# Expert blocks that finish their own rows: the combination stage of a fused RWKV and mixture-of-experts layer moved into the loop over blocks

## The chip, the cores and the metric

One core of a Trainium2 chip runs the whole layer in one launch. The metric is the device time of that core in microseconds (us); lower is better. Engines: PE multiplies matrices, DVE (VectorE), ACT (ScalarE) and POOL (GpSimd) work on tiles of 128 partitions, SP only issues transfers.

## The reference, cut to what matters

`x` is 2 x 2048 x 256 in fp32, there are 8 experts with two matrices each (256x1024, 1024x256), and each token goes to its 2 best experts.

```python
x = _layernorm(x + attn(x))                      # WKV scan over time, projections
logits = einsum('bsd,de->bse', x, Wg) + bg
s, idx = top_k(logits, 2);  s = softmax(s)
h = einsum('td,edf->etf', tokens, W1) + b1       # even experts gelu, odd experts silu
y = einsum('etf,efd->etd', a, W2) + b2
out = einsum('te,etd->td', comb, y)              # comb: the two weights, 0 elsewhere
x = _layernorm(x + out)
```

## The kernel before, in words

**Stage A** walks over 8 chunks of 2 x 256 tokens. PE projects, DVE scans over time, ACT makes the exponents and gates, POOL writes the rows out. For every chunk DVE picks the two best experts of each token (`choose`), PE ranks the picks and DVE works out the slots (`place`); ACT normalises x1 into a record (`normalise_x1`), SP stores x1 (`x1_dram`) and POOL sends each token's record twice by indirect transfer, once into the region of each expert (`send_records`). A record is x1 (256 columns), a label that tells the row of the result, and the slot of the second pick.

**Block stage.** Regions are cut into blocks of 256 records. Two blocks of expert 0 run before the count is known (`early_products`); a small table on DVE (`row_t`, `ex_t`, `par_t`, `full_t`, after `cnt_done`) tells the others. Up to 41 blocks are possible, 35 are used with this input. For each block ACT loads the records, PE transposes them (`turn_records`), multiplies by W1 (`product1`, 48 matmuls), ACT applies gelu or silu, DVE makes the lower parts (`lower_parts`), PE multiplies by W2 (`product2`, two halves of 24 matmuls; the second is left out for a block with at most 128 records). Numbers are split in an upper and a lower part (fp32r), three matmuls for each product. At step t PE does `turn_records(t+2)`, `product1(t+1)`, `product2(t)`. DVE at step t: `outputs(t-1)` adds b2 and writes `y_sb`, then `halves(t+2)`, `lower_parts(t+1)`. POOL scatters the two halves of `y_sb` to `expert_out_dram` and, when an expert's last block is through, splits the weights of the expert after next (`split`, L576 and L580) into its slot of `wx`. ACT, DVE and POOL run this in a counted loop with a tail of branches, PE unrolled.

**Combination stage.** When all blocks are out, SP loads 16 pieces of 2 x 128 tokens, both expert outputs side by side; DVE and ACT weigh and add them to x1, DVE takes the statistics, POOL the inverse root, ACT normalises, SP stores.

All order is written by hand: each engine's queue is in order, and semaphores join them. The two places that matter most, DVE's step and the wait in PE's step:

```python
def block_step(t):        # DVE
    outputs(t - 1, expert); halves(t + 2, ...); lower_parts(t + 1)
...
pe.wait_ge(aTl_done, t.upto(FC // 2))            # PE, ahead of product2(t)
after(pe, y_done, (t - 1).upto(BH))
```

Of the kernel before, what the change touches and what calls it, by code (L numbers as in the profile page):

```python
# [23 lines left out]
ALU = mybir.AluOpType  # L24
# [8 lines left out]
P = 128  # L33
# [50 lines left out]
def build(nc, x, decay, first, mix_k, mix_v, mix_r, wkT, wvT, wrT, woT, w1, b1, w2, b2, wgT, bg, out):  # L84
# [18 lines left out]
    LOWER = 8  # L103
    REGION = TOKENS + BLK
    DUMMY = E * REGION
    REC = C + 2
# [3 lines left out]
    PIECES = T // P  # L110
# [8 lines left out]
    ys = nc.dram_tensor("expert_out_dram", (2 * TOKENS, C), F32, kind="Internal").ap()  # L119
    x1d = nc.dram_tensor("x1_dram", (B, T, C), F32, kind="Internal").ap()  # L120

    with ExitStack() as ctx:
# [31 lines left out]
        top2 = sb("top2", [P, NCH, J, 2])  # L154
        score = sb("score", [P, NCH * J, 2])
        score_t = sb("score_t", [P, NCH * J, 2])
# [47 lines left out]
        m8 = sb("m8", [P, J, 8], F32, phase_a)  # L204
        i8 = sb("i8", [P, J, 8], U32, phase_a)
# [44 lines left out]
        xx = sb("xx", [P, PIECES, B, C])  # L250
        phase_b = ExitStack()
        b2_b = sb("b2_b", [P, E * C], F32, phase_b)
        recs = [sb(f"recs{n}", [P, BH, REC], F32, phase_b) for n in range(RING)]
        dest = [sb(f"dest{n}", [P, BH], I32, phase_b) for n in range(RING)]
# [4 lines left out]
        y_sb = [sb(f"y_sb{n}", [P, BH, C], F32, phase_b) for n in range(RING)]  # L259
# [4 lines left out]
        yy = [sb(f"yy{n}", [P, B, 2 * C]) for n in range(RING)]  # L264
        zz = [sb(f"zz{n}", [P, B, C]) for n in range(RING)]
        res = [sb(f"res{n}", [P, B, C]) for n in range(RING)]
        y2 = [sb(f"y2_{n}", [P, B, C]) for n in range(RING)]
        stats_c = [sb(f"stats_c{n}", [P, B, 6]) for n in range(RING)]
        mv_c = [sb(f"mv_c{n}", [P, B, 2]) for n in range(RING)]
        rstd_c = [sb(f"rstd_c{n}", [P, B]) for n in range(RING)]  # L270
        shift_c = [sb(f"shift_c{n}", [P, B]) for n in range(RING)]

# [3 lines left out]
        bias1_done, top2_done = sem("bias1_done"), sem("top2_done")  # L276
# [27 lines left out]
        known, dest_done, rows_clear = sem("known"), sem("dest_done"), sem("rows_clear")  # L304
# [5 lines left out]
        y_out = [sem(f"y_out{n}") for n in range(RING)]  # L310
# [3 lines left out]
        mm2_done, y_done = [sem(f"mm2_done{n}") for n in range(BH)], sem("y_done")  # L314
        exp_done, score_done = sem("exp_done"), sem("score_done")
        yy_in = [sem(f"yy_in{n}") for n in range(RING)]
        res_out = [sem(f"res_out{n}") for n in range(RING)]
        xx_in, y2_done, c_sum2 = sem("xx_in"), sem("y2_done"), sem("c_sum2")
        c_sum, c_bn, c_mv, c_var, c_rstd, c_res = (sem(n) for n in ("c_sum", "c_bn", "c_mv", "c_var", "c_rstd", "c_res"))

        REC_DMAS = 2 * J * 16
        ROUTE1, ROUTE2 = 2 * J + 3, 7
# [6 lines left out]
        def blocks_in_line(body):  # L329

            for n in range(EARLY, BLOCKS + 1):
                body(Step(None, n, RING, BLOCKS))

        LAST = ALWAYS // RING * RING

        def blocks(eng, body):

            plain = lambda n: Step(None, n, RING, BLOCKS)
            for n in range(EARLY, RING):
                body(plain(n))  # L340
            with eng.Fori(1, LAST // RING) as m:
                for n in range(RING):
                    body(Step(m, n, RING, BLOCKS, LAST // RING))
            for n in range(LAST, BLOCKS + 1):
                body(plain(n))
# [7 lines left out]
        def if_used(eng, used, u):  # L353

            return eng.If(used > u.number) if u.largest >= ALWAYS else nullcontext()

        def pieces(eng, body):

            for n in range(RING):
                body(Step(None, n, RING, PIECES))  # L360
            with eng.Fori(1, PIECES // RING) as m:
                for n in range(RING):
                    body(Step(m, n, RING, PIECES))

# [1159 lines left out]
```

## Time and profile before

| | us |
|---|---|
| median of 3 runs (lowest, highest) | 746.29 (745.2, 747.39) |
| the profiled execution, its own time | 746.1 |
| its span, first to last instruction | 744.4 |
| busy in it: PE, DVE, ACT, POOL | 634.5, 458.6, 393.5, 304.6 |
| mean granted clock of PE | 0.926 |
| stage A until | about 265 |
| first block product starts | 265.0 |
| last matmul ends | 684.7 |

The busy share of an engine is a mean over stages with different limits, so it tells little alone. One reads which engine is never idle in a stage, and on which chain of waits the stage ends. A groups row gives busy time and mean length of one instruction; a timeline row gives start and length, and in brackets the idle time before and what ended it.

### The profile page before, as it was taken

Reading aid. Unit: us, or ns where it says so; the run is one execution under the profiler, and the core shown is the slowest. Engines: PE = TensorE matmul, PEld = TensorE weight load, DVE = VectorE, ACT = ScalarE, POOL = GpSimd, SP = SyncE. Lnnn points to the kernel's source line nnn. Section 1 sums busy time; section 2 is a strip of 40 time slices with the busy share of each in tenths; the row PEclk is TensorE's granted clock in tenths of the full one; section 3 lists DMA queues with packets and bytes.
Section 4 is the critical chain, followed back from the end, with each engine's and each line's share of the span. In section 5 each row is a group of like instructions: output and inputs, shape, how many; then the busy total and the mean of one; then the engine's idle time right before and its main releaser. Section 6 shows DMA issues by size and latency. Waiting matters only on the chain.

```text
span 744.4 us, 14706 instructions
## 1 busy us (share of the span) xinstructions
PE 634.5 (85%) x4472; PEld 592.7 (80%) x4472; DVE 458.6 (62%) x963; ACT 393.5 (53%) x715; POOL 304.6 (41%) x353
## 2 busy tenths in 40 slices
PE   5969799999974688999999999999999999997000
PEld 4858678788763588999999999999999999997000
DVE  4748879999999465564474654454544454432684
ACT  3545566676574151655454636646455463642474
POOL 5110115456446668255191461371821632122363
PEclk9998899999986789999999999999999999999555
DMA  8400212321224655934114151141151111100793
GB/s 253 131 29 1 85 39 98 106 100 58 82 91 130 200 180 134 350 98 158 44 44 165 35 164 38 48 142 60 36 171 45 38 44 52 37 28 31 260 307 119
DMA packets 57116, 78.75 MB, mean 106 GB/s; under 512 B 5190, under 2 KB 46611, under 8 KB 56884
## 3 DMA queue, kind: packets, MB, share of 16 engines
q1 hardware_dynamic: 41540, 51.59, 21.8%
q0 software_dynamic: 6496, 16.99, 6.4%
q10 hardware_dynamic: 8976, 8.72, 4.3%
q8 instruction: 73, 1.20, 0.7%
q14 instruction: 31, 0.25, 0.1%
HBM read 49.14 MB, written 28.92 MB: 105 GB/s over the span
## 4 chain that ended last, share of the span: by engine, by line
PE 72%; DVE 11%; issue 6%; ACT 5%; DMA 2%; POOL 2%; SPq 0%; ACTq 0%; DVEq 0%; POOLq 0%
PE hT_ps L869 27%; PE y_ps L878 26%; PE vr_ps L722 7%; PE k_ps L722 7%; PE xT_ps L887 2%; PE wo_ps L730 2%; DVE o_all L1214 2%; DMA yy<-expert_out_dram 1%; DVE xl L1292 1%; ACT L1017 1%; PE small_ps L744 1%; POOL rstd_c L689 1%; PE xT_ps L790 1%; DVE nd L1221 1%; ACT r L1017 1%
## 5 line engine op out<-in xcount | busy, mean ns | idle before, releaser
L869 PE MATMUL hT_ps<-xTh,wx 128*128 128x256 f32 x1120 | 211.3, 287 | 1.0 <-issue 1.0
L878 PE MATMUL y_ps<-wx,aTh 128*128 128x256 f32 x1088 | 198.7, 284 | 0.9 <-DVE y_sb L1200 0.9
L869 PEld LDWEIGHTS hT_ps<-xTh,wx 128*128 128x128 f32 x1120 | 178.2, 193 | 1.3 <-issue 1.2
L878 PEld LDWEIGHTS y_ps<-wx,aTh 128*128 128x128 f32 x1088 | 170.7, 193 | 1.1 <-issue 1.1
L1192 DVE TENSOR_TENSOR aTl<-hT_ps,aTh 128x512 fp32r<-128x512 f32 x140 | 93.1, 688 | 120.2 <-ACT aTh L1080 120.2
L670 POOL DMA_INDIRECT expert_out_dram<-y_sb,dest x70 | 68.3, 976 | 240.2 <-DVE y_sb L1200 224.5
L869 PE MATMUL hT_ps<-xTl,wx 128*128 128x256 f32 x560 | 159.1, 284 | 0.0
L878 PE MATMUL y_ps<-wx,aTl 128*128 128x256 f32 x544 | 154.5, 284 | 0.0
L1074 ACT ACT_TABLE_LOAD x33 | 42.3, 1283 | 170.8 <-PE hT_ps L869 159.9
L1074 ACT ACTIVATE hT_ps<-hT_ps,b_c 128x256 f32<-128x256 f32 x280 | 113.9, 469 | 19.7 <-DVE dest L1182 15.7
L869 PEld LDWEIGHTS hT_ps<-xTl,wx 128*128 128x128 f32 x560 | 108.3, 193 | 0.0
L878 PEld LDWEIGHTS y_ps<-wx,aTl 128*128 128x128 f32 x544 | 104.9, 193 | 0.0
L635 POOL DMA_INDIRECT records_dram<-rec,slot_i x64 | 74.9, 1170 | 62.3 <-DVE rec L1338 32.6
L722 PE MATMUL vr_ps<-xh,wq 128*128 128x512 f32 x256 | 85.6, 406 | 0.0
L1080 ACT ACTIVATE aTh<-hT_ps 128x512 fp32r<-128x512 f32 x140 | 84.2, 648 | 0.0
L1200 DVE TENSOR_TENSOR y_sb<-y_ps,b_b 128x256 f32<-128x256 f32 x70 | 29.3, 424 | 79.6 <-PE y_ps L878 77.7
L580 POOL TENSOR_TENSOR wx<-staging,wx 128x512 fp32r<-128x512 f32 x56 | 70.3, 1298 | 0.6
L722 PE MATMUL k_ps<-xh,wq 128*128 128x512 f32 x128 | 47.9, 448 | 16.0 <-DVE nd L1221 14.2
L722 PEld LDWEIGHTS vr_ps<-xh,wq 128*128 128x128 f32 x256 | 49.1, 192 | 11.3
L722 PE MATMUL vr_ps<-xl,wq 128*128 128x512 f32 x128 | 51.3, 401 | 0.0
L722 PEld LDWEIGHTS k_ps<-xh,wq 128*128 128x128 f32 x128 | 28.0, 219 | 24.1 <-issue 17.3
L730 PE MATMUL wo_ps<-wo,newton 128*128 128x256 f32 x128 | 34.1, 414 | 7.5 <-DVE newton L1242 5.0
(194 smaller groups left out, 850.0 us busy)
## 6 DMA issues: line engine op xcount, KB each, us to landing
staging<-in_L_ffn_W SPq DMA_DIRECT2D x16, 1024.0 KB
recs<-records_dram ACTq DMA_DIRECT2D x33, 258.0 KB, 2.8
yy<-expert_out_dram SPq DMA_DIRECT2D x16, 512.0 KB, 5.7
xin<-in_L_attn_x SPq DMA_DIRECT2D x16, 256.0 KB, 4.2
xres<-in_L_attn_x SPq DMA_DIRECT2D x16, 256.0 KB, 3.1
x_dram<-rec SPq DMA_DIRECT2D x16, 256.0 KB, 3.5
xx<-x_dram SPq DMA_DIRECT2D x2, 2048.0 KB, 22.1
out<-res SPq DMA_DIRECT2D x16, 256.0 KB, 4.0
```

The lines of the kernel that those rows point to most:

```text
L580: pool.tensor_tensor(wx[:, e % 2, 1, at], raw[:, at], wx[:, e % 2, 0, at].bitcast(F32), ALU.subtract).then_inc(weights_ready if n == LOWER ...
L635: pool.indirect_dma_start(xs, bass.IndirectOffsetOnAxis(ap=slot_i[at][:, n:n + 1], axis=0), rec[at][:, j, :], None, bounds_check=DUMMY - 1 ...
L670: pool.indirect_dma_start(ys, bass.IndirectOffsetOnAxis(ap=dest[t.slot][:, h:h + 1], axis=0), y_sb[t.slot][:, h, :], None, bounds_check=2 ...
L722: ins = pe.matmul(out_ps.rearrange("p (b t) -> p b t", b=B), wq[:, mat, now, part, cc, oc * P:(oc + 1) * P], xpart[c.slot][:, cc, :, now:n ...
L730: ins = pe.matmul(wo_ps[:, h, :], mixed[:, cc, b, h * P:(h + 1) * P], wo[:, cc, :], start=cc == 0, stop=cc == CC - 1)
L869: ins = pe.matmul(hT_ps[b][:, f, :], wx[:, s, part, off:off + P], xpart[t.slot % 2][:, cc, :], start=k == 0, stop=k == len(terms) - 1)
L878: ins = pe.matmul(y_ps[h], apart[t.slot % 2][:, fc, h * P:(h + 1) * P], wx[:, s, part, off:off + C], start=k == 0, stop=k == len(terms) - 1)
L887: ins = pe.transpose(xT2_ps[:, cc, h * P:(h + 1) * P], recs[u.slot][:, h, cc * P:(cc + 1) * P], ident[:])
L1074: act.activation(hT_ps[b][:, f, :], hT_ps[b][:, f, :], func, bias=b1_c[:, bass.ds(expert * FC + (2 * b + f), 1)]).then_inc(act_done, 1)
L1080: act.activation(aTh[u.slot % 2][:, 2 * b - 2:2 * b, :], hT_ps[b - 1][:], ACT.Copy).then_inc(aTh_done, 1)
L1192: dve.tensor_tensor(aTl[u.slot % 2][:, 2 * b:2 * b + 2, :], hT_ps[b][:], aTh[u.slot % 2][:, 2 * b:2 * b + 2, :].bitcast(F32), ALU.subtract ...
L1200: dve.tensor_tensor(y_sb[u.slot][:, h, :], y_ps[h], b2_b[:, bass.ds(expert * C, C)], ALU.add).then_inc(y_done, 1)
```

## The change

The combination goes away as a stage. A record now carries both slots' information and both weights (261 columns): label, first slot, the larger of the two slots, and two sigmoids of the score gap, made by ACT in stage A (`weigh`). A block's rows whose partner lies in a later block (`where_to[0]`) have their share, 2 x weight x (y + b2) + x1, stored to `x1_dram` by indirect transfer; rows whose partner was earlier (`where_to[1]`) gather the partner's share, add it, and are normalised with 4 x eps and scattered to `out`. The weight splits move from POOL to ACT (upper parts, 4 pieces) and DVE (lower parts, 4 pieces), behind the activations of an expert's first block. The counted loops are unrolled, and unused blocks lie in one nest of branches.

```diff
-    REC = C + 2
+    REC = C + 5
-    ys = nc.dram_tensor("expert_out_dram", (2 * TOKENS, C), F32, kind="Internal").ap()
...
+        def blocks_in_line(eng, used, lag, body):
+            with ExitStack() as needed:
+                for n in range(EARLY, BLOCKS + lag):
+                    if n - lag >= ALWAYS:
+                        needed.enter_context(eng.If(used > n - lag))
+                    body(Step(None, n, RING, BLOCKS))
...
@@ POOL
-            split(1)
+            for n in range(RING):
+                pool.memset(other[n][:], 0.0).then_inc(others_clear, 1)
...
+            def spread_z(t):
+                pool.wait_ge(mv_z_done, since_second(t) * BH)
...
+            def keep_shares(t):
+                pool.wait_ge(marks, t.upto(8))
+                pool.wait_ge(share_done, t.upto(BH))
...
+            def gather(t):
+                pool.wait_ge(marks, t.upto(8))
+                pool.wait_ge(share_out[(t - 1).slot], (t - 1).turn(16 * BH, 16 * BH))
...
+            def block_step(t):
+                for stage, u in ((keep_shares, t - 1), (send_rows, t - 2), (gather, t), (spread_z, t - 1)):
...
@@ PE
-                pe.wait_ge(y_done, early_block(0).upto(BH))
+                pe.wait_ge(share_done, early_block(0).upto(BH))
...
-                        after(pe, y_done, (t - 1).upto(BH))
+                pe.wait_ge(share_done, (t - 1).upto(BH, 1))
...
+                pe.wait_ge(share_done, (t - 1).upto(BH))
@@ ACT
+            def weigh(c):
+                at = c.number % RECS
+                act.wait_ge(gap_done, c.upto(1))
+                scattered(act, c)
+                act.activation(rec[at][:, :, C + 3], gap[:], ACT.Sigmoid, scale=-1.0).then_inc(weighed, 1)
+                act.activation(rec[at][:, :, C + 4], gap[:], ACT.Sigmoid).then_inc(weighed, 1)
...
+                if (i - 3).exists and i.number < NCH:
+                    weigh(i - 3)
                 if i.exists:
                     exponents(i)
...
+            def split_upper(t):
...
+                    act.wait_ge(raw_in, expert * 32 + 64)
+                    take_wait(act)
+                    for n in range(SPLITS):
...
+                        act.activation(wx[:, bass.ds(slot, 1), 0, at].rearrange("p a b -> p (a b)"), raw[:, at], ACT.Copy).then_inc(hi_done, 1)
...
@@ DVE
+            def mark(u, own):
...
+                dve.tensor_tensor(is_top[n][:], rows[:, :, C + 1], own, ALU.is_equal).then_inc(marks, 1)
...
+            def share_half(u, h, expert):
...
+                dve.tensor_tensor(y_ps[h], y_ps[h], b2_b[:, bass.ds(expert * C, C)], ALU.add).then_inc(y_done, 1)
+                dve.wait_ge(y_done, u.upto(BH, h + 1))
+                dve.scalar_tensor_tensor(out=share[u.slot][:, h, :], in0=y_ps[h], scalar=weight[u.slot][:, h:h + 1],
+                                         in1=recs[u.slot][:, h, 0:C], op0=ALU.mult, op1=ALU.add).then_inc(share_done, 1)
...
+            def add_other(u):
+                dve.wait_ge(other_in[u.slot], in_ring(u) * 16 * BH)
...
+                dve.tensor_tensor(row_out[u.slot][:], share[u.slot][:], other[u.slot][:], ALU.add).then_inc(sum_done, 1)
...
+            def normalise(u):
+                dve.wait_ge(rstd_z_done, since_second(u))
...
+                    dve.tensor_scalar(row_out[u.slot][:, h, :], row_out[u.slot][:, h, :], mv_z[u.slot][:, h, 0:1],
+                                      rstd_z[u.slot][:, h:h + 1], ALU.subtract, ALU.mult).then_inc(row_done, 1)
```

DVE's new step t is: second half of `share_of(t-1)`, `halves(t+2)` and `mark(t+2)`, `normalise(t-2)`, `lower_parts(t+1)`, `add_other(t-1)`, first half of `share_of(t)`, `split_lower(t)`. DVE in the block stage, one step of the kernel before:

```order
L1446 TENSOR_LOAD ex_t
L1446 ISA x2
L1199 REGISTER_ALU
L1200 ISA
L1200 TENSOR_TENSOR y_sb<-y_ps,b_b 128x256 x2
L1174 REGISTER_ALU
L1176 CAST xTh<-xT_ps 128x512
L1178 TENSOR_TENSOR xTl<-xT_ps,xTh 128x512
```

and the same place of the change, from the end of the marks to the start of the split (`TENSOR_LOAD` brings a number of a table into a register of the engine):

```order
L1181 SCALAR_TENSOR_TENSOR weight<-recs,twice 128x2
L1228 TENSOR_SCALAR row_out<-row_out,mv_z,rstd_z 128x256 x2
L1188 TENSOR_TENSOR aTl<-hT_ps,aTh 128x512 x4
L1216 TENSOR_TENSOR row_out<-share,other 128x512
L1219 BN_STATS stats_z<-row_out 128x6 x2
L1223 BN_AGGR mv_z<-stats_z 128x2 x2
L1209 TENSOR_LOAD ex_t
L1209 ISA x2
L1203 ISA
L1203 TENSOR_TENSOR y_ps<-y_ps,b_b 128x256
L1205 SCALAR_TENSOR_TENSOR share<-y_ps,weight,recs 128x256
L1494 TENSOR_LOAD split_t
```

Five kinds of work now stand in DVE's queue between two blocks where one stood, and there are three table loads in a step instead of one. ACT in stage A, chunks 3 to 7, the change:

```order
L940 ACTIVATE v<-vr_ps 128x512 x2
L969 ACT_TABLE_LOAD
L969 ACTIVATE rec<-gap 128x4
L970 ACTIVATE rec<-gap 128x4
L945 ACTIVATE B<-nd 128x4x256
L946 ACTIVATE A<-nd 128x4x256
L948 ACT_TABLE_LOAD
L948 ACTIVATE B<-B 128x4x256
```

Before, `B<-nd` followed `v<-vr_ps` directly and there was no table load ahead of `B<-B`: two table loads and two small activations are new, between the values and the exponents. DVE at the start of the block stage, the change, behind the lower parts of block 1 (12 more links of the table stand ahead of these, at L1461 to L1472, and 8 marks behind each `xTl`):

```order
L1203 TENSOR_TENSOR y_ps<-y_ps,b_b 128x256
L1205 SCALAR_TENSOR_TENSOR share<-y_ps,weight,recs 128x256
L1484 TENSOR_TENSOR wx<-staging,wx 128x1024 x4
L1188 TENSOR_TENSOR aTl<-hT_ps,aTh 128x512 x4
L356 TENSOR_LOAD ends
```

The lower weights of expert 1 were POOL's before; they now stand ahead of the lower parts of block 2.

## Rows read from the trace of the kernel before

**Rows 1.** Busy time by stretch: us, then each engine, clock, DMA share, GB/s.

```profile
300.00:685.00 385.00, 382.85 (x3200) 382.20 (x3198) 189.93 (x323) 204.12 (x422) 147.53 (x121) 1.00 0.27 86
684.80:744.40 59.60, 0.00 (x0) 0.00 (x0) 36.72 (x113) 30.55 (x64) 26.98 (x65) 0.54 0.66 218
```

**Rows 2.** The chain that ended last, in order of time: start, us, what.

```profile
300.86 5.76 PE hT_ps L869 x48
...
576.94 5.76 PE y_ps L878 x48
...
582.70 0.44 PE xT_ps L887 x4
...
686.07 2.29 DMA expert_out_dram<-y_sb,dest
```

**Rows 3.** Timeline of DVE, one block of the steady stage.

```profile
571.23 0.69 DVE L1176 CAST xTh<-xT_ps 128x512 fp32r<-128x512 f32 x1
...
572.56 0.34 DVE L1182 SCALAR_TENSOR_TENSOR dest<-recs,own_f 128x1 int32<-128x1 f32 x2
...
578.56 1.29 DVE L1192 TENSOR_TENSOR aTl<-hT_ps,aTh 128x512 fp32r<-128x512 f32 x2 [0.53 <-ACT aTh L1080]
580.03 0.42 DVE L1200 TENSOR_TENSOR y_sb<-y_ps,b_b 128x256 f32<-128x256 f32 x1 [0.18 <-PE y_ps L878]
```

**Rows 4.** Timeline of DVE in the combination stage.

```profile
696.41 0.74 DVE L1482 BATCH_NORM_STATS2 stats_c<-zz 128x6 f32<-128x256 f32 x2
697.08 0.67 DVE L1476 TENSOR_TENSOR zz<-zz,y 128x512 f32<-128x512 f32 x1
697.67 0.24 DVE L1490 BATCH_NORM_AGGREGATE mv_c<-stats_c 128x2 f32<-128x6 f32 x2
```

**Rows 5.** Timeline of DVE at the start of the block stage.

```profile
278.15 0.50 DVE L1417 TENSOR_TENSOR past_s<-past_s,rowbase 128x328 f32<-128x328 f32 x1
...
281.41 0.19 DVE L1429 TENSOR_SCALAR ex_t<-ex_f 128x41 int32<-128x41 f32 x1
...
281.93 2.48 DVE L1192 TENSOR_TENSOR aTl<-hT_ps,aTh 128x512 fp32r<-128x512 f32 x4
...
304.12 0.76 DVE L1200 TENSOR_TENSOR y_sb<-y_ps,b_b 128x256 f32<-128x256 f32 x2 [0.88 <-issue]
```

**Rows 6.** Timelines of ACT, then of DVE, in stage A.

```profile
164.43 0.60 ACT L973 ACTIVATE v<-vr_ps 128x512 f32<-128x512 f32 x1 [2.21 <-PE vr_ps L722]
...
189.35 0.60 ACT L973 ACTIVATE v<-vr_ps 128x512 f32<-128x512 f32 x1 [1.68 <-PE vr_ps L722]
190.87 1.07 ACT L978 ACTIVATE B<-nd 128x1024 f32<-128x1024 f32 x1 [0.92 <-DVE nd L1221]
...
169.44 1.22 DVE L1276 TENSOR_TENSOR b2v<-B,v 128x1024 f32<-128x1024 f32 x1
...
195.82 1.22 DVE L1276 TENSOR_TENSOR b2v<-B,v 128x1024 f32<-128x1024 f32 x1
```

**Rows 7.** Groups of POOL by line: count, busy us, mean ns, idle before.

```profile
L635 POOL DMA_INDIRECT records_dram<-rec,slot_i x64 | 74.9, 1170 | 62.3 <-DVE rec L1338 32.6 <-issue 25.0 <-DMA recs<-records_dram 3.8
...
L670 POOL DMA_INDIRECT expert_out_dram<-y_sb,dest x70 | 68.3, 976 | 240.2 <-DVE y_sb L1200 224.5 <-issue 15.3
...
L689 POOL TENSOR_TENSOR rstd_c<-var_e,half_neg 128x2 f32<-128x2 f32 x16 | 11.1, 696 | 1.3
```

**Rows 8.** Timeline of POOL: slow indirect issues of stage A, and two splits.

```profile
225.02 1.88 POOL L635 DMA_INDIRECT records_dram<-rec,slot_i  x1 [0.30 <-issue]
...
326.65 3.64 POOL L576 TENSOR_SCALAR wx<-staging 128x4096 fp32r<-128x4096 f32 x1
...
374.44 3.63 POOL L576 TENSOR_SCALAR wx<-staging 128x4096 fp32r<-128x4096 f32 x1
```

**Rows 9.** Timeline of ACT in the steady block stage.

```profile
572.74 1.28 ACT L1074 ACT_TABLE_LOAD   x1 [5.67 <-PE hT_ps L869]
...
577.86 1.16 ACT L1080 ACTIVATE aTh<-hT_ps 128x512 fp32r<-128x512 f32 x2
```

More of the change, by code:

```diff
@@ L351, in blocks_in_use, with if_used @@
             return eng.value_load(ends[0:1, E - 1:E], min_val=ALWAYS, max_val=BLOCKS)
[L353 to L363, printed above, removed]
-        def column(i, b, k):
-            at = (i.off // TH * J + b * TH + i.off % TH) * 2 + k
-            return at if i.fixed else i.m * (i.every // TH * J * 2) + at
+        def if_used(eng, used, u, known=0):
+            return eng.If(used > u.number) if u.number >= max(ALWAYS, known) else nullcontext()
         def after(eng, semaphore, value):
@@ new lines, in send_rows @@
+            def send_rows(t):
+                pool.wait_ge(row_done, since_second(t) * BH)
+                take_wait(pool)
+                for h in range(BH):
+                    pool.indirect_dma_start(
+                        rows_2, bass.IndirectOffsetOnAxis(ap=where_to[t.number % MARKS][:, 1, h:h + 1], axis=0),
+                        row_out[t.slot][:, h, :], None, bounds_check=TOKENS - 1, oob_is_err=False).then_inc(out_done[t.slot], 16)
+            keep_shares(early_block(0))
+            def block_step(t):
+                for stage, u in ((keep_shares, t - 1), (send_rows, t - 2), (gather, t), (spread_z, t - 1)):
+                    if u.exists and (with_second(u) or stage is keep_shares):
+                        with if_used(pool, used, u, t.number - 1):
+                            stage(u)
@@ L1452, in block_step @@
+                u = t - 2
+                if u.exists and with_second(u):
+                    with if_used(dve, used, u, known):
+                        normalise(u)
                 u = t + 1
                 if u.exists:
-                    with if_used(dve, used, u):
+                    with if_used(dve, used, u, known):
                         lower_parts(u)
-            blocks(dve, block_step)
-            dve.wait_ge(xx_in, 16 * B)
-            flat = score[:].rearrange("p n k -> p (n k)")
@@ L1492, in out_step @@
-            def out_step(i):
-                for stage, c in ((first_sum, i), (statistics, i - 1), (second_sum, i), (means, i - 1)):
-                    if c.exists:
-                        stage(c)
-            pieces(dve, out_step)
-            last = Step(None, PIECES - 1, RING, PIECES)
-            statistics(last)
-            means(last)
+                u = t - 1
+                if u.exists and with_second(u):
+                    with if_used(dve, used, u, known):
+                        add_other(u)
```

439 lines of the change are left out of this document (219 added, 220 removed).

## The prediction

> **What bounds the kernel now.** I read the busy times by stretch first, then the chain of waits, then the timelines of the engines that serve PE. Between 300 and 685 us PE works 382.85 of 385 us at full granted clock, while DVE has 189.93, ACT 204.12 and POOL 147.53 us of work [rows 1]: the block stage is PE's own time. The chain there runs through PE alone, and one block is 5.76 us of first product, 5.76 of second and 0.44 of transposes, 11.96 us (11.95 from block to block, as the starts in the chain say) [rows 2]. From the last matmul at 684.7 to the end at 744.4 PE has nothing to do: 59.6 us in which DVE, ACT, POOL and the transfers combine and normalise [rows 1]. That is what the change attacks. In stage A DVE is the engine that is hardly ever idle, so whatever is late there shows.
>
> **Part 1, the tail.** Removed: the 59.6 us. In its place stands what is still open when PE ends, with the last two blocks, 33 and 34. I count from the end of block 33's second product, at 677.9 in this trace (66.5 us before the end). In the kernel before, the last block then waited 0.9 us for `y_sb`; now only its second half waits for a share, so PE ends at about 5.9 instead of 6.8. POOL is the engine with the queue: an indirect issue is 0.98 us [rows 7] and 0.30 to the next ([rows 8] shows that gap), 1.28 each, two per stage. After block 33's share (1.3) it starts at about 2.2: keep_shares(33) to 4.8, send_rows(32) to 7.3, gather(34) behind the landing of the stores (about 2.3 us, [rows 2]) to 9.9, spread_z(33) (about 1.2, the power being 0.70, [rows 7]) to 11.2. The gather has landed by 12.2; DVE adds and takes statistics until 14.1. Then keep_shares(34) to 13.8, send_rows(33) to 16.3, spread_z(34) to 17.6, DVE normalises to 18.2, send_rows(34) issues to 21.3 and lands at 23.6. In the trace the last instruction ends some time after the last landing; I allow 1.7 us and get 25.3. 66.5 - 25.3 = **41.2 us saved**. Bounds: 30 us if each stage of POOL's queue takes 1.5 times as long, 46 if stages that I put in a row overlap.
>
> **Part 2, the steady block.** PE's matmuls are the same. The question is whether the engines that serve it keep within 11.95 us. DVE per block: two shares, each an addition of 0.42 [rows 3], 0.1 until its result is known, and a weighted addition of the same size, together 1.9; halves 1.33 (from the cast at 571.23 to the next operation at 572.56, [rows 3]); 8 marks on 2 columns at 0.12 each, as two small operations take 0.34 [rows 3], 1.0; normalisation, two of at most 0.42, say 0.6; four lower parts back to back 2.48 [rows 5]; adding the partner's share 0.67, statistics 0.74 and 0.24 with a wait, 1.8 [rows 4]. Sum **9.1 us**. Three loads of a register from a table are extra: mostly hidden, as 0.18 us of idle time before `y_sb` holds one [rows 3]; 0.88 us for two, where nothing hides them [rows 5]. So 9.1 to 10.4. ACT: a table load and activations from 572.74 to 579.0 [rows 9], 6.3 us, unchanged. POOL: six issues of 1.28 and 1.2 for the root, 8.9. All under 11.95: 0 us.
>
> An expert's split now costs ACT a table load of 1.28 and four copies of 128x1024 at about 1.07 [rows 6], 5.6 us, and DVE four subtractions of 1.22 [rows 6], 4.9, plus up to 1.3 for loads. There are six in the loop, 47.8 us or four blocks apart [rows 8]. In such a step DVE ends the split some 17 us after the step's start and the second share at 18.2; PE wants it at 21.0, and wants the lower parts of the block after next at 24.3 and has them by 23.7. Over four blocks DVE needs 4 x 9.1 + 4.9 = 41.3 us, at worst 4 x 10.4 + 6.2 = 47.8, of 47.8. So again **0 us**, and the cover is just used up at the worst end: if a DVE step takes 10.9, four blocks take 49.8, 2 us over, for six experts 12 us less what PE's slack hides.
>
> What goes away on POOL, the splits of 3.64 us and eight more pieces, held nothing on PE's chain: 0.
>
> **Part 3, stage A.** ACT's `weigh` stands between the copies of v and the exponents: 1.28 for the sigmoid's table [rows 9], about 0.3 for two tiny activations, and 1.28 more before the exponents. DVE's multiplication with the exponents starts at 195.82 and 169.44 [rows 6]. From 189.95 (v copied) the new order gives 191.5 for the start of `B<-nd`, two passes of 0.97, a table load and 1.05, so 195.8: just in time. In the other chunk v is copied at 165.03 and the exponents are there at 170.9, 1.5 us late. Of the five chunks two are like this one (1.5 and 0.8 by the same walk), three cost 0.1. With one more small operation on DVE per chunk (0.1): **+3.3 us**; bounds 0 (the copies of v slip ahead) and 8 x 1.6 = 13 (every chunk pays).
>
> **Part 4, the start of the block stage.** Marks of block 1 stand ahead of the last `choose`: 1.1 us, of which idle time covers half, +0.6. After the lower parts of block 1 (end 284.4, [rows 5]) DVE makes 12 more table steps: five of 246 elements at 0.44 (from 0.50 for 328, [rows 5]), seven small at 0.22 with their wait ([rows 5]: 0.19), 3.8 us; then two shares instead of two additions, to 290.1. Block 1's second product starts then, 2.8 us later than before. Behind it come the marks, the halves of block 3 (299.3), a share, the split of expert 1 (4.9 us, to 306.1) and only then the lower parts of block 2, the first at 306.8. PE's first product of block 3 started at 300.86 [rows 2] and needs that bank: 306.85. **+6.0 us**, and 0.5 for a lower clock after the idle time. ACT has by then made the upper parts (4.3 us in a gap that the pads' transfers leave open). Bounds 3 and 12.
>
> **The sum.** 744.4 - 41.2 + 3.3 + 0.6 + 6.5 = 713.6 us of span; the time is 1.7 over the span, **715 us**. The profiled execution (746.1) lies 0.2 under the median. Change: -31 us, -4.2%. A measurement of this kernel tells 0.3% (2.2 us) from no change.
>
> **The rivals.**
>
> *DVE becomes the bound, in part.* For: DVE's queue grows from about 6 to over 9 us a block, each step has three register loads and several waits on its own results, and a split comes on top. Against: its operations are timed above. At 10.9 us a step and 0 slack, 11 us are lost: 726. If every load cost 0.88 as in the idle row of [rows 5], 11.8 a step, four blocks with a split take 53.4, 5.6 over, six times, 34 us: 749, no gain.
>
> *POOL's queue becomes the bound: slower than before.* Six indirect issues a block instead of two, on an engine whose issues were 1.88 us while DVE worked on large operands in SBUF [rows 8], and 1.17 in the mean in stage A against 0.98 in the block stage, where DVE read PSUM [rows 7]. DVE now has additions, statistics and normalisations on SBUF in this stage. At 1.88 + 0.30 each and 1.2 for the root a block takes 14.3 us on POOL, 2.3 over PE's, for 32 blocks 75 us: 790. It decides from 11.95; it makes the kernel slower from 12.9 us a block. Against: DVE's SBUF operations are some 3 us of a block, not all of it, and gathers and scatters have 9 us of slack. The Trainium skill ("SBUF — State Buffer", section "Who interferes with whom") says that GpSimd and VectorE share one port pair as an exclusive lock, so that descriptors of transfers issued by GpSimd wait out a two-port VectorE operation. By that rule some issues lengthen by one such operation each, which speaks for this rival in kind; the rows of stage A agree in direction.
>
> *The weights come late.* The split moved from the end of an expert to ACT's and DVE's queues; if both fall behind, PE waits at each of six changes of expert, up to the 5 us of a split each: 745. Against: with four or five blocks per expert PE asks for them three steps later.
>
> The Trainium skill also has a price for a table switch ("ScalarE: Activation LUTs", section "What ACT_TABLE_LOAD costs"): 1283 ns and a drain of about 1380 ns, 2.66 us in all. The trace shows 1.28 and the next activation directly behind it [rows 9]. By the page's figure each of the two switches in stage A would cost 1.4 us more, some 14 us over five chunks, and the result would be 729.
>
> **How the numbers follow.** PE stays the bound, 705 to 722: 0.62. DVE partly the bound or the start dearer, 722 to 742: 0.22. Weights late, or DVE at its upper bound (745 to 749): 0.05. POOL the bound: 0.07. Something below 705: 0.04. The range, 706 to 738, leaves out half of that last one, the far end of the second case and the two dear rivals, about 0.19. Faster by over 0.3%: 0.87. Within 0.3%: 0.03. Slower: 0.10.
>
> **What would show it.** Right: PE busy without a gap between about 312 and 694 us, blocks 11.95 apart; under 20 us from the last matmul to the end; DVE at 75 to 90% in that stage; `weigh` costing at most 2 us in a chunk; first product of block 3 near 311. Wrong: PE waits for `share` or `aTl` in most blocks (DVE bound), `other` waited for by DVE and POOL never idle (POOL bound), waits at the first block of each expert (weights).

## The result, and the profile after

The changed kernel takes 774.43 us (median of 4 runs, 770.35 to 775.89) against 746.84 for the kernel before beside it (745.2 to 749.0): a ratio of **1.036, interval 1.031 to 1.041**. It is slower. The forecast was 715, range 706 to 738, with 0.87 on faster. The profiled execution took 775.44 us, its span 773.6, mean clock 0.906. In two of the five groups of runs below everything took longer, the kernel before included (753.0 and 755.5 us instead of 744 to 747); these runs are marked "disturbed", and every ratio is against the kernel before of the same group.

The busy time by stretch, columns as in [rows 1]:

```profile
300.00:685.00 385.00, 347.83 (x2774) 341.04 (x2774) 269.53 (x714) 209.58 (x398) 182.28 (x205) 0.94 0.25 78
685.00:749.00 64.00, 60.59 (x506) 59.19 (x504) 43.24 (x118) 28.79 (x61) 37.29 (x43) 1.00 0.19 54
749.00:773.60 24.60, 0.00 (x0) 0.00 (x0) 4.08 (x11) 0.00 (x0) 11.38 (x14) 0.60 0.12 40
```

The tail behaves: 24.6 us behind the last matmul where 59.6 stood. But PE, which never paused between 300 and 685 us before, now works 347.8 of 385 us, part of it at a lower clock. What PE waits for from 300 us on (us in total, times, longest), from the list of waits:

```profile
PE xT_ps L857 <- DMA recs<-records_dram: 32.7, 10, 6.0
PE hT_ps L839 <- issue: 3.8, 10, 0.7
PE hT_ps L839 <- DVE aTl L1188: 2.1, 1, 2.1
PE y_ps L848 <- DVE share L1205: 1.4, 1, 1.4
```

Neither DVE nor POOL is named much. Ten waits, eight of them of 1.4 to 6.0 us and two under 0.4, are for the **load of the records**, of which the prediction says nothing. ACT's timeline at the first of the six splits in the loop (start, us; in brackets the idle time before):

```profile
344.61 1.16 ACT L1058 ACTIVATE aTh<-hT_ps 128x512 fp32r<-128x512 f32 x2
345.47 0.39 ACTq L1044 DMA_DIRECT2D recs<-records_dram  x1
348.06 1.28 ACT L1083 ACT_TABLE_LOAD   x1 [2.29 <-issue]
349.35 3.90 ACT L1083 ACTIVATE wx<-staging 128x1024 f32 x4
353.27 1.28 ACT L1052 ACT_TABLE_LOAD   x1
...
358.40 1.16 ACT L1058 ACTIVATE aTh<-hT_ps 128x512 fp32r<-128x512 f32 x2
359.28 0.39 ACTq L1044 DMA_DIRECT2D recs<-records_dram  x1
```

and the chain of waits right behind it:

```profile
359.28 7.89 DMA recs<-records_dram
367.21 1.11 PE xT_ps L857 x4
```

The load is issued at 359.28, takes 7.89 us instead of about 3, and PE starts its transposes at 367.21. They take 1.11 us instead of 0.44 [rows 2], since the clock has fallen. The granted clock of the idle stretch, of the transposes and of the first 3 us of the product behind them (last column but two) is 0.78, then 0.50, the lower of its two levels, 1.2 GHz:

```profile
361.20:367.20 6.00, 0.01 (x1) 0.00 (x0) 3.80 (x10) 0.00 (x0) 1.76 (x3) 0.78 0.72 244
367.20:368.30 1.10, 1.08 (x4) 0.71 (x4) 0.92 (x2) 0.00 (x0) 1.02 (x1) 0.50 0.00 0
368.30:371.30 3.00, 2.99 (x15) 2.96 (x15) 2.77 (x12) 0.00 (x0) 2.47 (x4) 0.50 0.09 25
```

The eight first products behind the waits of 1.4 to 6.0 us, and one behind the wait of 2.1 us for lower parts, take 7.1 to 8.0 us instead of 5.9.

The change also moves the load within ACT's step, which the excerpt of the diff ahead of the prediction does not show:

```diff
 def block_step(t):          # ACT
-    u = t + 3
-    ...
-            after(act, dest_done, (u - RING).upto(BH))
-            load_records(u)
     u = t + 1
     ...
             activate_block(u)
+    u = t + 3
+    ...
+            after(act, share_done, (u - RING).upto(BH))
+            load_records(u)
+    split_upper(t)
```

In both traces a load follows directly on an activation, so ACT's timeline looks the same. The difference is which block it carries. Before, the load behind the activation of block k was for block k+3, which PE turns 15.5 us after the issue; now it is for k+2, turned one block of 11.95 us sooner, some 3.5 us after the issue. A landing takes 2.8 us in the median before, so there is next to nothing left for a late ACT or a busy transfer.

Of the feared costs, the groups show little (busy us, mean ns, idle before):

```profile
L631 POOL DMA_INDIRECT x_dram<-share,where_to x70 | 72.7, 1038 | 162.1 <-issue 147.2
L642 POOL DMA_INDIRECT other<-x_dram,where_to x64 | 67.7, 1057 | 39.0 <-issue 39.0
L651 POOL DMA_INDIRECT out<-row_out,where_to x64 | 62.8, 981 | 22.7 <-issue 16.8
L1203 DVE TENSOR_TENSOR y_ps<-y_ps,b_b 128x256 f32<-128x256 f32 x70 | 30.2, 431 | 56.6 <-issue 52.9
```

POOL's indirect issues are 0.98 to 1.06 us, where [rows 7] had 0.98. DVE stands 52.9 us ahead of 56 shares, 0.94 us each: loading the expert's number is not hidden, though I had taken it as mostly hidden.

### The profile page after: what moved, and what is told of

Same layout as the page of the kernel before. It is cut to its first block, busy times and chain, and to the rows that moved or that the text cites. A ratio compares the mean times of both kernels' runs of the same rounds, so it can differ in the third digit from the quotient of the medians.

```text
span 773.6 us, 14838 instructions
## 1 busy us (share of the span) xinstructions
PE 659.2 (85%) x4472; PEld 608.2 (79%) x4472; DVE 550.3 (71%) x1398; ACT 414.1 (54%) x709; POOL 352.8 (46%) x424
## 3 DMA queue, kind: packets, MB, share of 16 engines
q1 hardware_dynamic: 28708, 34.85, 13.8%
## 4 chain that ended last, share of the span: by engine, by line
PE 50%; ACT 14%; issue 13%; DVE 9%; DMA 7%; ACTq 3%; POOL 1%; SPq 0%; POOLq 0%; DVEq 0%
PE hT_ps L839 17%; PE y_ps L848 12%; PE vr_ps L692 8%; DMA recs<-records_dram 7%; PE k_ps L692 6%; ACT hT_ps L1052 5%; PE wo_ps L700 3%; PE xT_ps L857 2%; PE small_ps L714 2%; ACT aTh L1058 2%; ACT wx L1083 2%; DVE o_all L1242 1%; ACT L1052 1%; DVE xl L1320 1%; PE xT_ps L760 1%
## 5 line engine op out<-in xcount | busy, mean ns | idle before, releaser
L839 PE MATMUL hT_ps<-xTh,wx 128*128 128x256 f32 x1120 | 222.5, 297 | 6.3 <-issue 3.8
L848 PE MATMUL y_ps<-wx,aTh 128*128 128x256 f32 x1088 | 194.4, 281 | 4.4 <-DVE share L1205 4.4
L839 PEld LDWEIGHTS hT_ps<-xTh,wx 128*128 128x128 f32 x1120 | 187.1, 202 | 11.9 <-issue 9.3
L839 PE MATMUL hT_ps<-xTl,wx 128*128 128x256 f32 x560 | 164.6, 294 | 0.0
L631 POOL DMA_INDIRECT x_dram<-share,where_to x70 | 72.7, 1038 | 162.1 <-issue 147.2
L1052 ACT ACTIVATE hT_ps<-hT_ps,b_c 128x256 f32<-128x256 f32 x280 | 113.7, 465 | 20.4 <-PE hT_ps L839 18.7
L839 PEld LDWEIGHTS hT_ps<-xTl,wx 128*128 128x128 f32 x560 | 113.4, 202 | 0.0
L642 POOL DMA_INDIRECT other<-x_dram,where_to x64 | 67.7, 1057 | 39.0 <-issue 39.0
L651 POOL DMA_INDIRECT out<-row_out,where_to x64 | 62.8, 981 | 22.7 <-issue 16.8
L1203 DVE TENSOR_TENSOR y_ps<-y_ps,b_b 128x256 f32<-128x256 f32 x70 | 30.2, 431 | 56.6 <-issue 52.9
L857 PE MATMUL xT_ps<-ident,recs 128*128 128x128 f32 x132 | 22.7, 300 | 34.8 <-DMA recs<-records_dram 34.8
```

The costliest lines, as they stand in the source:

```text
L631: pool.indirect_dma_start(rows_1, bass.IndirectOffsetOnAxis(ap=where_to[t.number % MARKS][:, 0, h:h + 1], axis=0), share[t.slot][:, h, :], ...
L642: pool.indirect_dma_start(other[t.slot][:, h, :], None, rows_1, bass.IndirectOffsetOnAxis(ap=where_to[t.number % MARKS][:, 1, h:h + 1], ax ...
L651: pool.indirect_dma_start(rows_2, bass.IndirectOffsetOnAxis(ap=where_to[t.number % MARKS][:, 1, h:h + 1], axis=0), row_out[t.slot][:, h, : ...
L839: ins = pe.matmul(hT_ps[b][:, f, :], wx[:, s, part, off:off + P], xpart[t.slot % 2][:, cc, :], start=k == 0, stop=k == len(terms) - 1)
L848: ins = pe.matmul(y_ps[h], apart[t.slot % 2][:, fc, h * P:(h + 1) * P], wx[:, s, part, off:off + C], start=k == 0, stop=k == len(terms) - 1)
L857: ins = pe.transpose(xT2_ps[:, cc, h * P:(h + 1) * P], recs[u.slot][:, h, cc * P:(cc + 1) * P], ident[:])
```

## The experiments

There were eighteen runs. Labels in brackets are those of the disturbed ones. All edits of a disturbed run were run again undisturbed, but for f1 and f2.

| run | edit | ratio [interval] |
|---|---|---|
| c0 | the changed kernel again | 1.039 [1.035, 1.043] |
| c3 | kernel before, load behind the activation | 1.049 [1.046, 1.052]; disturbed (e3): 1.056 |
| e7 | kernel before, loops unrolled | 1.001 [0.998, 1.003] |
| e6 | changed, weights' transfer cut to 8 KB pieces | 1.003 [1.001, 1.005] |
| e5 | changed, split cut to 8 columns | 1.013 [1.010, 1.016] |
| c4 | changed, no sigmoid | 1.032 [1.029, 1.034]; disturbed (e4): 1.107 |
| d1 | changed, load first | 1.120 [1.115, 1.125]; disturbed (e1, c1): 1.124, 1.125 |
| f1 | changed, six buffers | disturbed: 1.123 |
| c2 | load first and six buffers | 0.980 [0.976, 0.984]; disturbed (e2): 1.036 |
| f2 | c2 and one register load a block | disturbed: 1.031 |
| b1 | f2, start mended, sigmoid moved | 0.977 [0.974, 0.979] |
| d2 | b1 without the moved sigmoid | **0.957 [0.954, 0.960]**; disturbed (b2): 1.025 |

**A control (c0).** The changed kernel, unaltered, since the first four runs (e1 to e4) had been disturbed.

> The changed kernel itself, unaltered, beside the three runs that follow. Reason: in the four runs before this one the kernel before took 753 us instead of 747, and ScalarE and VectorE stood idle for 1.5 to 3.8 us at places where nothing they need was missing, which the changed kernel's first trace does not show. If that is a matter of where the program's instructions lie (each edit moves them), this run looks like the first one: ratio 1.03 to 1.04, no such idle stretch. If it is a matter of the chip that ran them, the ratio is above 1.06 here too, and the runs before must be read against this one.

1.039, with 31.8 us of waits for records in ten places and no idle stretch without a cause: the first result repeats. That the disturbance does not come from where the instructions lie is shown by the programs that ran both ways (e3 and c3, e4 and c4, e2 and c2, b2 and d2).

**The move alone, in the kernel before (c3).** The three statements of the diff above change places, nothing else.

> The kernel before with the load of records behind the activation, again, for the same reason. In the first call it was 1.0555, with 18.8 us of PE waits for records in ten places. Theory: on an undisturbed chip the waits remain, since they come from the order alone: at the changes of expert, where the weights' transfer shares the way, and after blocks with at most 128 records; 1.01 to 1.04. If it is 1.00, the order costs nothing in the kernel before, and the loss of the changed kernel needs the split in front of the load as well.

Measured 781.67 us against 744.41, 37 us more. PE's waits from 300 us on:

```profile
PE xT_ps L887 <- DMA recs<-records_dram: 18.7, 9, 3.9
PE hT_ps L869 <- issue: 6.2, 12, 0.7
```

This is more than I expected (1.01 to 1.04), and more than the net loss of the changed kernel. By their places they come at the start (a landing of 6.7 us, issued at 305.47), at the changes of expert and behind half blocks. The waits are 25 us; most of the rest is five first products of 7.5 to 8.2 us and slow transposes behind them. So the split on ACT is not needed for a loss of this kind; the order does it.

**Unrolled code (e7).** A rival formed after the result: the loops of ACT and DVE are written out block by block, and instructions run once must be fetched.

```diff
-            with eng.Fori(1, LAST // RING) as m: ...
+            for n in range(EARLY, BLOCKS + 1):
+                body(Step(None, n, RING, BLOCKS))
```

> Another part of the change alone, in the kernel before: the counted loops of ScalarE and VectorE over the blocks are written out block by block (ScalarE's program grows from 1382 to 2786 instructions, VectorE's from 1076 to 1442). Theory A (the load of records one step late, and the loop of waits behind it, is the whole loss): no difference, within 0.5% of the kernel before, and no PE wait over 1 us. Rival theory B (instructions that are executed once must be fetched, and the engines stand while they are: the changed kernel's programs for ScalarE and VectorE are 3784 and 3463 instructions long): idle stretches of 1.5 to 3.8 us marked as issue or as an unknown releaser appear on ScalarE and VectorE inside a block, PE loses some of them where they come late in a block, and the kernel is 1 to 5% slower.

744.76 against 745.19: nothing, and no PE wait over 0.9 us from 300 us on. The fetches are there, as the page's queue rows show (packets, MB, share), of the kernel before, of this run, of the changed kernel:

```profile
q14 instruction: 31, 0.25, 0.1%
```

```profile
q14 instruction: 45, 0.37, 0.2%
```

```profile
q14 instruction: 63, 0.52, 0.2%
```

The fourteen more of the second row cost nothing, in straight code. The Trainium skill ("Runtime: NRT & Kernel Launch", section "Instruction fetch mechanics") says so too: fetching is sequential and mostly hidden, and a taken branch out of the window is what stalls. This trace agrees as to the first half.

**What lengthens the landing (e6).** The raw weights of experts 3 to 7 are loaded as two pieces of 8 KB instead of two of 1 MB, so this kernel leaves out most of them.

```diff
+                if e > 2:
+                    for n in range(2):
+                        sp.dma_start(raw[:, 16*n:16*n+16], w1[e][0:P, 0:16]).then_inc(raw_in, 16)
+                    return
```

> The changed kernel, with the two 1 MB loads of each expert's raw weights, from expert 3 on, cut to 8 KB each (so the weights that are split are not those experts'). Theory A: the weights' transfer is what makes the landing of the records take 7 to 8 us instead of 3.2 in the steps that follow a split; the six waits of about 6 us shrink to about 1.5, and with the clock that comes back the kernel gets 25 to 35 us faster than the run of the changed kernel beside it. If the landing stays at 7 us or the waits stay, the transfer is not what delays it, and ScalarE's late issue behind the split is the cause by itself: under 10 us.

746.08 us, 27 less than the changed kernel beside it (772.96). From issue to landing of the records, first the changed kernel, then this run:

```profile
DMA to landing us min/median/max: 2.7/3.4/7.7
```

```profile
DMA to landing us min/median/max: 2.7/2.9/3.8
```

and PE's waits fall from 31.8 us to

```profile
PE xT_ps L861 <- DMA recs<-records_dram: 12.1, 10, 2.5
```

The 2 MB of weights are asked for when DVE ends its split, three microseconds ahead of the late load (356.60 and 359.28 at the first split), and the two meet: in the changed kernel the five loads behind such a transfer land after 6.0 to 7.9 us. This is within the expectation.

**What the split itself costs (e5).** All pieces of the split, on ACT and DVE, cut from 1024 to 8 columns, so most of the weights are not split.

```diff
-                        at = bass.ds(n * WE // SPLITS, WE // SPLITS)
+                        at = bass.ds(n * WE // SPLITS, 8)
```

> The changed kernel, with every piece of the six splits in the block stage cut from 1024 to 8 columns on ScalarE and VectorE (the weights that are not split are left as they were before; the branches, loads of numbers and table loads of the split stay). Theory A: 3.9 us less in ScalarE's queue and 4.6 in VectorE's at each of six experts, so the load of the records after a split goes out 3.9 us earlier, but collides with the raw weights' transfer as before: the waits of 6 us fall to 2 to 3, 15 to 25 us faster than the changed kernel beside it. If the kernel gets less than 6 us faster, the splits on these two engines cost nothing, as part 2 of the prediction had it.

754.33 us, 18.6 less than the changed kernel: within the expectation. The waits for records are 17.0 us in 8 places. The cut works in two ways that this run does not separate. At the first split the load of the records goes out at 357.38 instead of 359.28, and it lands in 6.26 us instead of 7.89, the weights being asked for at 353.09 instead of 356.60.

**The load first (e1, c1, d1), buffers (f1), both (e2, c2).** The load's place is undone:

```diff
+                load_records(t + 3)          # with its wait
                 activate_block(t + 1)
-                load_records(t + 3)
                 split_upper(t)
```

> One part undone: in ACT's step the load of the records for three blocks ahead stands ahead of the activation of the next block again, as it does in the kernel before; everything else is the changed kernel. Theory (the load is issued too late: PE waits 32.7 us for records in the block stage and then pays again in clock): the load is issued about 6 us earlier in each step, so nearly all waits of xT_ps for records should go, 32.7 us down to under 10, and the time should fall from 774 to about 725 to 740; some is left because the load now waits on ACT for a share that DVE finishes late in a split step. Rival (DVE and ACT are the bound through splits and register loads): PE would wait for hT or share instead, and the time would stay above 765. Rival (the records wait for memory that other transfers hold): landings stay near 8 us in split steps, waits of 2 us at each of six experts, about 755.

This fell: 1.124 and 1.125 in the disturbed e1 and c1, far slower. The trace of e1 gave a ring of waits, which I then forecast for an undisturbed run:

> The load first with four buffers. If the ring of waits (activation, last lower part, partner's sum, two shares, load) holds, most blocks are 14.6 us apart whatever the time of day: ratio 1.07 to 1.10 against an undisturbed kernel before. If it comes out at 0.98 to 1.0, the ring closes only under disturbance, and four buffers do.

836.58 us against 745.02, ratio 1.120, dearer than forecast. ACT's timeline in d1, one round:

```profile
743.00 0.39 ACTq L1044 DMA_DIRECT2D recs<-records_dram  x1
744.18 1.28 ACT L1052 ACT_TABLE_LOAD   x1 [8.34 <-issue]
...
749.29 1.16 ACT L1058 ACTIVATE aTh<-hT_ps 128x512 fp32r<-128x512 f32 x2
757.59 0.39 ACTq L1044 DMA_DIRECT2D recs<-records_dram  x1
```

and DVE's in the same round:

```profile
750.10 1.29 DVE L1188 TENSOR_TENSOR aTl<-hT_ps,aTh 128x512 fp32r<-128x512 f32 x2 [0.52 <-ACT aTh L1058]
751.30 0.68 DVE L1216 TENSOR_TENSOR row_out<-share,other 128x512 f32<-128x512 f32 x1
752.02 0.75 DVE L1219 BATCH_NORM_STATS2 stats_z<-row_out 128x6 f32<-128x256 f32 x2
...
755.92 0.43 DVE L1203 TENSOR_TENSOR y_ps<-y_ps,b_b 128x256 f32<-128x256 f32 x1 [1.08 <-issue]
756.39 0.48 DVE L1205 SCALAR_TENSOR_TENSOR share<-y_ps,weight,recs 128x256 f32<-128x256 f32 x1
```

From load to load 14.59 us: activation, last lower part, partner's sum, statistics, two shares, load. Since the share now reads `recs`, its buffer comes free a good part of a block later than before, when `dest_done` freed it at once. With four buffers a load ahead of the activation must wait for it, and the activation behind it too. The ring is 14.6 us in a block without a split, and about 20 in each of the six with one, which the forecast of 1.07 to 1.10 had left out. So the late place was no oversight that one can simply undo: **the change took away the slack of the buffers, and the moved load pays for it.** The buffers alone (f1), with the load still late:

> The changed kernel with six buffers of records and the load still behind the activation. Theory (the place of the load is the cause; the buffers only make it possible): the share of four blocks back is long done when a load behind the activation asks for it, so the buffers change nothing: 1.034 to 1.040, waits for records 31 to 33 us in ten places. If the time falls by more than 5 us, the wait for the share did hold loads back.

It ran only disturbed, 1.123, with 51.8 us of waits for records in 19 places; the changed kernel with copies in place of the sigmoid (e4, disturbed) had 48.4 in 20 places and 1.107. It shows no gain; that it costs nothing was not shown. Both edits together:

```diff
-                        after(act, share_done, (u - RING).upto(BH))
+                        after(act, share_done, (u - 6).upto(BH))
-    recs[u.slot] ... rec_in[u.slot]
+    recs[u.number % 6] ... rec_in[u.number % 6]
```

> The changed kernel with the load of records ahead of the activation and six buffers of records, as in the first call, whose chip took 753 us for the kernel before and let ScalarE and VectorE stand for 2 to 4 us with nothing missing. Here, if the kernel before takes 742 to 748 us: theory (the late load is the loss): no wait of PE for records, none of those idle stretches, block stage at 11.7 to 12 us a block but for the start; last matmul near 707 to 712, about 732 to 738 us, ratio 0.98 to 0.99. Rival (the register loads and splits of VectorE would be the bound once the records are on time): waits for share and aTl in most blocks, ratio above 1.01 as in the first call (1.0355).

729.42 against 744.41, 0.980. PE's waits from 290 us on:

```profile
PE y_ps L850 <- DVE share L1207: 12.3, 6, 3.0
PE hT_ps L841 <- DVE aTl L1190: 2.9, 2, 2.1
PE xT_ps L859 <- DMA recs<-records_dram: 2.3, 1, 2.3
```

The loss is gone, some 44 us of it. Of the six waits for shares, four stand at splits (0.7, 1.9, 2.5 and 3.0 us, 8.1 in all); the others are one of 2.7 us in the first blocks and one of 1.4 in the last.

**Stage A (c4).** The two weights are copies of the gap, so this kernel leaves the sigmoid out.

```diff
-                act.activation(rec[at][:, :, C + 3], gap[:], ACT.Sigmoid, scale=-1.0)
-                act.activation(rec[at][:, :, C + 4], gap[:], ACT.Sigmoid)
+                act.activation(rec[at][:, :, C + 3], gap[:], ACT.Copy, scale=-1.0)
+                act.activation(rec[at][:, :, C + 4], gap[:], ACT.Copy)
```

> The changed kernel with copies of the gap in place of its sigmoid (no table loads for the two weights of a share in stage A; the weights of the shares are the part that differs from the reference), again. Against the changed kernel on an undisturbed chip (ratio 1.036 to 1.039, first block product 4 to 6 us later than in the kernel before). If the table loads are what stage A pays, as part 3 of the prediction has it (+3.3 us), the first block product starts about 3 us earlier than there and the ratio falls to 1.032 to 1.035. If the start does not move, stage A pays for something else.

768.35 against 744.41, 1.032, against 1.036 and 1.039. The first block product starts at 266.7 us; in seven undisturbed traces with the sigmoid at 268.4 to 271.3 (mean 270.3), in three with the old stage A at 262.7 to 265.0 (mean 264.0). So eleven table loads cost about 3.5 us, and the rest of the new stage A about 2.7. The prediction had 3.9 for both. The first of the two rests on one trace of c4, beside traces that differ by 2.9 us among themselves; the ratio, lower by 0.004 to 0.007, agrees.

**All mended (b1, f2, d2).** On top of c2: one load of the expert's number a block, behind the normalisation; expert 1's lower weights behind `lower_parts(2)`; and in b1 `weigh(i-3)` behind `gates(i+1)`.

```diff
 def step(i):                # ACT, stage A; in b1 alone
-    weigh(i - 3)             # stays here for the last chunk
     exponents(i)
     ...
     gates(i + 1)
+    weigh(i - 3)
 ...
 def block_step(t):          # DVE; f2, b1, d2
     normalise(t - 2)
+    expert_of[t] = dve.value_load(ex_t[t])
     lower_parts(t + 1)
...
+            lower_parts(early_block(2))       # b1, d2
             for n in range(SPLITS): ...       # expert 1's lower weights
-            lower_parts(early_block(2))
```

The register load alone (f2):

> Six buffers, load first, and VectorE loading an expert's number once a block behind the normalisation. The run with six buffers waited 12.3 us for shares in six places, at splits, and showed 51 us of idle time of VectorE ahead of the shares, 0.94 each. Theory (VectorE is at its limit only in the steps with a split: part 2's cover is just used up at the worst end): 8 to 10 us faster than 729, with under 4 us of waits for shares left: 719 to 722, ratio 0.966 to 0.971. If it stays above 727, the gain of the run with all edits came from the start of the block stage.

It ran only disturbed, 1.031, so its expectation stays untested by itself; the three together:

> Six buffers and the load first, as above, and three more edits: in stage A the sigmoid for the weights stands right behind the gates, whose table it uses (two table loads less in four chunks); VectorE loads an expert's number once a block, behind the normalisation, not twice ahead of the shares; expert 1's lower weights are made behind the lower parts of block 2. By theory: 3 us from stage A, 5 to 6 us at the start of the block stage, and nothing from the register loads unless VectorE is the bound: 722 to 730 us, ratio 0.965 to 0.98. If VectorE bounds the run with six buffers, the single load gives 0.9 us for each of 32 blocks more.

727.06, 0.977, in the expected range, but by luck, since two errors cancel: its block stage was almost without a wait behind the first blocks, better than the forecast had it, and its first block product came at 284.2, some 14 us later than in the others. The waits of POOL and ACT between 60 and 285 us say why:

```profile
POOL records_dram L592 <- ACT rec L972: 43.2, 4, 17.2
```

```profile
ACT rec L1003 <- POOL shift L571: 45.6, 6, 9.4
```

POOL sends a chunk's records ahead of the inverse root of a later chunk. With the weights late, POOL waits, the root is late, ACT's normalisation waits. Eight table loads are saved (28 before 290 us instead of 36), and 14 us are lost (727.06 against 712.92 without the edit):

> Six buffers, the load first, one register load a block, expert 1's lower weights behind the lower parts of block 2; stage A as the change has it. If the kernel before takes 741 to 748 us here: first block product near 270, block stage periodic at 11.73 us, 712 to 716 us, ratio 0.957 to 0.962. If the kernel before takes above 750 us, the time is disturbed again and the ratio comes out near the 1.025 of the last call.

**712.92 us against 745.02**: faster than both kernels. Its busy row from 300 to 685 us, the columns as above:

```profile
300.00:685.00 385.00, 382.77 (x3259) 382.09 (x3257) 311.70 (x830) 236.61 (x458) 221.83 (x247) 1.00 0.28 87
```

DVE has 311.7 us of work in 385 and ACT 236.6, more than in the changed kernel's row above in the same time, and PE hardly waits; full blocks are 11.7 us apart. All of PE's waits from 300 us on, neither of them at a split:

```profile
PE y_ps L850 <- DVE share L1207: 1.2, 1, 1.2
PE hT_ps L841 <- DVE aTl L1190: 0.9, 1, 0.9
```

## Why the prediction was wrong

By its own steps, with the spans of the first two profiled executions (773.6 - 744.4 = +29.2):

| step | predicted | measured |
|---|---|---|
| Part 3 and marks, until the first block product | +3.9 | +5.7 (265.03 to 270.70) |
| Part 4, until block 3's product | +6.5 | +5.6 (300.86 to 312.18, less 5.7) |
| Part 2, until block 33's second product ends | 0 | **+52.3** (377.0 to 429.3) |
| Part 1, from there to the end | -41.2 | -34.4 (66.5 to 32.1) |

**Part 2 is the step that failed**, in its sentence on ACT: "a table load and activations ..., 6.3 us, unchanged". I compared sums of work per engine with 11.95 us and took the place of the load in ACT's queue as given. The instructions and their times were indeed unchanged; one DMA issue had moved past an activation, and with it the distance from issue to use fell from 15.5 to 3.5 us. c3 shows that this alone loses 37 us in the kernel before. In the changed kernel the 52.3 us are 32.7 of waits for records, 3.8 of short gaps ahead of first products (1.0 before), 13.8 of slow first products and some 7 between the start of the transposes and the product, less 4 to 5 that the products gain (an undisturbed block takes 11.73 us instead of 11.95). The landings of 6.0 to 7.9 us that make five of the waits long come from the weights' transfer (e6). The split in the same queue makes the issue later by 1.9 us at the first of them (e5). These two gains overlap and are not to be added.

**The splits at 0 us.** Right only when the records are on time and the register loads are hidden: d2 makes all of them, and PE waits at none. Wrong behind a late load, where e5 gets 18.6 us back. "The cover is just used up at the worst end" was the true state of c2: with the register loads exposed (0.94 us each, taken as mostly hidden) PE waited 8.1 us for shares at four splits, and with them hidden d2 does not. Between the profiled spans of c2 and d2 lie 18.7 us, of which 11.7 come behind the start of block 4's first product, where the register load is the only edit left between the two.

**Part 1.** The mechanism held, the size was off by 6.8 us. The term is "1.7 us" from the last landing to the end. Transfers between 764 and 774 us in the changed kernel, and between 738 and 745 in the kernel before (40 slices each):

```profile
DMA  9101240000000000000000000000000000000000
```

```profile
DMA  9910007999500000000000000000000000000000
```

The last packets are at 765.7 and 739.9, the ends at 773.6 and 744.4: 7.9 us and 4.5, not 1.7. Of the 6.8 us this makes 6.2. Two instruction fetches (q14) fall between 764 and 765.2, as POOL leaves the nest of branches; that they are the cause was not tested.

**Parts 3 and 4** were right within 2 us, no better than the 2.9 us by which the first product's start differs among traces of the same stage A. With expert 1's lower weights behind `lower_parts(2)`, d2 has block 3's product 39.1 us after the first instead of 41.5 in c2, and block 4's 50.9 instead of 55.1: 4.2 us, most of the 4.9 that part 4 has for them.

**The rivals.** POOL's queue: fell; two of the three kinds of issues became 0.06 to 0.08 us longer and the third stayed the same, where the rival needed 0.9. With the lock that the Trainium skill describes ("SBUF — State Buffer", "Who interferes with whom") this agrees in sign alone. An estimate from the Trainium skill's price of a table switch ("ScalarE: Activation LUTs", "What ACT_TABLE_LOAD costs") would have made stage A 14 us dearer than my 3.3; c4 got back about 3.5. Weights late: not seen. DVE the bound in part: not in the changed kernel, true in c2, by 8.1 us of waits at splits and some 12 with what comes behind them. No rival held the one that came, and the slower side had 0.10.

The forecast of 715 lies near d2 (713), and this is luck. The change with the records on time and nothing else is c2, 729. Against the kernel before, by the four steps of the table, c2 has +6.2, +5.7, +6.0 and -34.0 us, and d2 +3.4, +3.2, -6.8 and -34.6, where the forecast had +3.9, +6.5, 0 and -41.2. In d2 the 6.8 us that the blocks gain, which I had not forecast, make up for a tail that is 6.6 us too dear. What was priced well are the tail's saving, within a fifth, and the two starts.

## What to carry to other kernels

When work is moved between stages, list for every transfer who issues it, behind what, for which block, and how long before its use; a busy sum cannot show a load that comes one turn late. A buffer that a later step still reads is held longer, and the load that waits for it holds what stands behind it: count buffers again before moving either. A wait on the engine that bounds the kernel costs more than its length: here about half as much again, most of it through the clock (c3: 25 us of waits, 37 lost).

## What the runs showed of the hardware

In the changed kernel a wait of PE of 1.4 to 6.0 us is followed by a first product of 7.1 to 8.0 us instead of 5.9, and waits of 4.4 us or more also by transposes of 1.11 instead of 0.44; behind waits of 0.25 and 0.37 us the product takes 5.9 as ever. Behind the wait that ended at 367.21 the granted clock stayed at 0.50 until about 371.3 and was 1.00 from 372.3. Over 300 to 685 us it was 0.94 where it had been 1.00.

In the disturbed runs engines stood idle although the trace shows nothing that they need as missing: DVE ahead of a share in e2 (load first, six buffers), ACT inside an activation in e4 (copies in place of the sigmoid):

```profile
461.11 0.43 DVE L1205 TENSOR_TENSOR y_ps<-y_ps,b_b 128x256 f32<-128x256 f32 x1 [2.96 <-remote]
```

```profile
510.82 0.86 ACT L1052 ACTIVATE hT_ps<-hT_ps,b_c 128x256 f32<-128x256 f32 x2 [3.07 <-remote]
```

The kernel before lost 1.1 to 1.4% by it, the best two 7 and 8% (779 and 771 us against 729 and 713). I suspected the fetching of unrolled code; but one such stretch of ACT, 3.7 us long and ending at 476.85 in e4, has no instruction fetch in it, and the cause stays open. A ratio from such a time says nothing of an edit: d2's program, 0.957 undisturbed, had 1.025 there.
